# Halving the last chunk of each block's gather in two graph-attention layers of a three-layer GNN kernel

## The chip, the cores and the metric

One core of a Trainium2 chip runs the whole program. The metric is the device time of one execution in microseconds (us).

## What is computed

The input is a graph of 6250 nodes with 256 features and 100000 edges (`src`, `dst`, sorted by `dst`). There are three attention layers: two layers of a transformer-like GNN without edge types ("untyped", layers 0 and 1), and one with 64 edge types ("typed", layer 2).

```
h = x @ w_in + b_in
for l in range(2):                                  # the untyped layers
    xn = layernorm(h)
    q, k, v = xn @ wq[l] + bq[l], ...               # 8 heads of 32
    scores = einsum('ehd,ehd->eh', q[dst], k[src]) * scale       # an edge list with self loops
    attn = softmax over the edges with the same dst
    agg = segment_sum(attn * v[src], dst)
    h = h + agg @ wo[l] + bo[l]
    h = h + gelu(layernorm(h) @ w1[l] + b1[l]) @ w2[l] + b2[l]
```

The typed layer adds a row per edge type to k[src], has 4 heads, no feed-forward part, and ends with a layer normalisation.

## The kernel before

The nodes are sorted by their number of incoming edges and cut into 49 blocks of 128, one node for each partition. A block needs as many **slots** as its fullest node has edges. Four slots are a **chunk** (CH = 4), six chunks at most are a **round** (CPS = 6); a block has one round, but for two blocks that have two. A chunk is always whole: with 17 edges on its fullest node a block gathers 20 slots.

GpSimd (POOL in the profile) gathers: `gather_round` issues one indirect DMA for each slot, which brings for each of 128 nodes the row of one neighbour from `kv_dram`, 256 words of K and 256 of V, 256 KB in all, into the tile `kv` (L1255). `kv` holds two rounds. A chunk's gather waits for `used` (TensorE has summed this chunk two rounds ago) and for `taken` (VectorE has seen this chunk of the round before land). GpSimd also fetches the block's own rows (`gather_nodes`, L1235) and scatters the finished K and V rows of block b - 5 into the next layer's table (`scatter`, L1219), ahead of block b's gathers; the scatter waits for `recq`, ScalarE's last copy into `rec_out` (L1747).

VectorE (DVE) then goes over the block three times. `scores`: for each chunk `landed(c)` waits for its DMAs and counts up `taken`; `products(c)` multiplies K by the query in place (L1319); `head_sums(c-1)` adds up the heads of the chunk before (L1324). `maxima` (L1374 to L1379) subtracts the maxima for ScalarE's exponential. Then come the residual and the statistics of blocks b - 1 and b - 2 (`second`, L1492 in layer 0, L1494 in layer 1, waits for the feed-forward sum `f2`), and `weigh` multiplies V by the weights in place, chunk by chunk (L1424).

TensorE (PE) adds V's slots up in PSUM: `sums` has a loop over the chunks, four matmuls with the identity in each (L1870; the profile has two rows for each matmul, and two weight loads on PEld), and L1873 closes the sum. In the next iteration follow the feed-forward matmuls of block b - 2 (`feed_forward`, L1945, 32 rows; `feed_out`, L1958), the projections, and again `sums`. ScalarE (ACT) takes the sums (L1638), does the eight gelus (`hidden`, L1710), the exponential, and the copies into the record (`record`, L1745 to L1747).

The engines run one iteration for each block, in program order, and meet at semaphores; no planner sorts anything. How many rounds and chunks a block has comes from a small table that the first part of the kernel works out on the chip, `block_table`, two words a block; every engine reads a word of its copy `block_row` at the start of an iteration (L397).

Of the kernel before, what the change touches and what calls it, by code (L numbers as in the profile page):

```python
# [29 lines left out]
KMAX = NB + E // W  # L30
TYPES = 64
# [42 lines left out]
class Passed:  # L74
# [7 lines left out]
    def wait(self):  # L82
        self.eng.reg_add(self.count, self.count, self.by)
        self.eng.wait_ge(self.semaphore, self.eng.snap(self.count, min_val=1))
# [19 lines left out]
def build(nc, x, src, dst, edge_type_64, w, out):  # L104

    with ExitStack() as ctx:
# [17 lines left out]
        block_table = dram("block_table", [NB, 2], I32)  # L124
# [30 lines left out]
        block_row = sb("block_row", [1, NB * 2], I32)  # L155
# [7 lines left out]
        w_qkv = [sb(f"w_qkv{l}", [P, KD, 3 * D]) for l in range(3)]  # L163
# [29 lines left out]
        prod = sb("prod", [P, D])  # L193
        acc = sb("acc", [P, D])
# [76 lines left out]
        bt_out = carve(2, I32)  # L271
# [93 lines left out]
        ]  # L365
        later_loads = [
# [12 lines left out]
        for c, k in enumerate("kvq"):  # L379
            later_loads.append((w_qkv[2][:, :, c * D:(c + 1) * D], of_rows(w[f"L1_gnn_W{k}"])))  # L380
        later_loads.append((w_o[2][:], of_rows(w["L1_gnn_Wo"])))


        class Blocks:
# [9 lines left out]
            def next(self, b):  # L394

                sl = slice(2 * b, 2 * b + 1) if isinstance(b, int) else bass.ds(2 * b, 1)
                both = self.eng.value_load(block_row[0:1, sl], min_val=1, max_val=KMAX * PACKED + CPS)  # L397
# [10 lines left out]
        class Later:  # L408
# [7 lines left out]
            def next(self, b):  # L416
                at = 2 * b + 1
                sl = slice(at, at + 1) if isinstance(b, int) else bass.ds(at, 1)
                earlier = self.eng.value_load(block_row[0:1, sl], min_val=0, max_val=KMAX - NB)
# [80 lines left out]
        with nc.Block() as block:  # L500
# [151 lines left out]
            def _(dve):  # L652
# [124 lines left out]
                def block_sizes():  # L777
# [12 lines left out]
                    ceil_div(b0[:, 3:4], b0[:, 2:3], CPS)  # L790

                    step(nc.vector.tensor_scalar(b0[:, 4:5], b0[:, 3:4], -1.0, -float(CPS), ALU.add, ALU.mult))
                    step(nc.vector.tensor_tensor(b0[:, 4:5], b0[:, 4:5], b0[:, 2:3], ALU.add))
                    step(nc.vector.tensor_scalar(b0[:, 5:6], b0[:, 3:4], -1.0, float(PACKED), ALU.add, ALU.mult))
                    nc.vector.tensor_tensor(bt_out[0:NB, 0:1], b0[:, 4:5], b0[:, 5:6], ALU.add)
# [283 lines left out]
        for l in range(3):  # L1079
# [46 lines left out]
            with nc.Block() as block:  # L1126
                @block.sync
                def _(sp):
                    if not typed:
                        sp.dma_start(w_1, of_rows(w["L0_gnn_w1"][l])).then_inc(s["wload"], 16)  # L1130
                        sp.dma_start(w_2, of_rows(w["L0_gnn_w2"][l])).then_inc(s["wload"], 16)
                    looked_up, scored = Passed(sp, s["to_exp"]), Passed(sp, s["scaled"])
# [76 lines left out]
                def _(pool):  # L1209
# [38 lines left out]
                    def gather_round(u, k, chunks_left):  # L1248
                        def gather(c):
# [4 lines left out]
                            for slot in range(c * CH, (c + 1) * CH):  # L1254
                                pool.indirect_dma_start(  # L1255
# [802 lines left out]
```

## Time and profile before

| | |
|---|---|
| median of three runs | 6420.99 us (6406.24 to 6423.1) |
| the profiled execution: its time | 6426.95 us |
| its span in the profile | 6424.9 us |
| gathers of neighbour rows (L1255) | 2616, 872 in each layer |
| busy: PE, DVE, POOL, ACT | 62%, 55%, 46%, 30% of the span |

The profiled execution's time is 2.0 us over its span and 6.0 us over the median of the runs. Times in rows are microseconds from the span's start, unless they are marked ns. "x26" is a number of instructions, "issue" is time in which the engine waited for nothing that the profile shows, and the name behind "<-" is what ended an idle stretch.

### The profile page before, as it was taken

How to read it: one execution, taken by the hardware profiler on the slowest of the kernel's cores; microseconds unless marked ns; L12 is line 12 of the kernel's file. 1: busy time of each engine (PE TensorE's matmuls, PEld its weight loads, DVE VectorE, ACT ScalarE, POOL GpSimd, SP SyncE). 2: the span in 40 equal slices, each digit the busy share in tenths (PEclk: the TensorE clock that was granted, in tenths of full speed). 3: DMA queues.
4: the chain of work that ended last, by engine and by line, in shares of the span. 5: the costliest groups of instructions: out<-in, count | busy, mean ns of one | idle time of the engine just before them, and what ended most of it. 6: DMA issues, size and time to landing. Idle time of an engine off the chain costs nothing. (4 is left out here: it accounts for less than half of the span.)

```text
span 6424.9 us, 95711 instructions
## 1 busy us (share of the span) xinstructions
PE 3987.0 (62%) x17667; PEld 2921.0 (45%) x17668; DVE 3509.8 (55%) x5215; ACT 1924.9 (30%) x4404; POOL 2952.8 (46%) x2969
## 2 busy tenths in 40 slices
PE   8555455665666666565466566666666456666665
PEld 6222344544454444444354454444445345545544
DVE  6431445655555444355465555444436567777775
ACT  3332232222222222332222222222234222333433
POOL 0230435545444444244554444444425466666664
PEclk9777677777777777777777777777787667777777
DMA  3333545555554444344555555444435456665553
GB/s 123 128 115 81 158 128 163 161 156 154 151 151 138 147 147 140 113 134 138 171 159 157 157 154 143 138 141 141 141 99 153 123 168 174 183 173 172 170 173 108
DMA packets 384172, 935.62 MB, mean 146 GB/s; under 512 B 143749, under 2 KB 156255, under 8 KB 384105
## 3 DMA queue, kind: packets, MB, share of 16 engines
q0 software_dynamic: 232080, 751.31, 40.9%
q1 hardware_dynamic: 151708, 182.79, 8.8%
q10 hardware_dynamic: 320, 0.84, 0.0%
q8 instruction: 18, 0.29, 0.0%
q14 instruction: 46, 0.38, 0.0%
HBM read 791.63 MB, written 143.30 MB: 146 GB/s over the span
## 5 line engine op out<-in xcount | busy, mean ns | idle before, releaser
L1255 POOL DMA_INDIRECT kv<-kv_dram,idx x2616 | 2600.3, 994 | 1397.4 <-issue 770.5
L1870 PE MATMUL ps_acc<-kv,ident 128*128 x5232 | 1288.1, 408 | 49.3 <-issue 39.1
L1870 PEld LDWEIGHTS ps_acc<-kv,ident 128*128 128x128 f32 x5232 | 1074.2, 207 | 259.3 <-issue 95.6
L1324 DVE TENSOR_REDUCE sc<-kv 128x32 f32 (+2 forms) x654 | 791.2, 1213 | 362.2 <-issue 347.0
L1945 PE MATMUL ps_big<-xnaT,w_ffn 128*128 128x128 f32 x3136 | 524.5, 301 | 620.1 <-issue 616.5
L1319 DVE TENSOR_TENSOR kv<-kv,ps_q 128x1024 f32 x654 | 785.6, 1214 | 201.4 <-issue 197.8
L1958 PE MATMUL ps_w<-w_ffn,shared 128*128 128x256 f32 x1568 | 557.2, 531 | 390.8 <-ACT shared L1710 339.9
L1424 DVE TENSOR_TENSOR kv<-kv,ps_q x654 | 753.8, 1215 | 45.7 <-issue 36.3
L1945 PEld LDWEIGHTS ps_big<-xnaT,w_ffn 128*128 128x128 f32 x3136 | 446.7, 209 | 662.9 <-issue 651.1
L1958 PEld LDWEIGHTS ps_w<-w_ffn,shared 128*128 128x128 f32 x1568 | 426.0, 279 | 543.0 <-ACT shared L1710 399.0
L1638 ACT COPY agg<-ps_acc 128x256 f32<-128x256 f32 x147 | 54.8, 373 | 1949.9 <-remote 1054.3
L1219 POOL DMA_INDIRECT kv_dram<-rec_out,scatter_to x98 | 100.4, 1025 | 829.9 <-issue 829.9
L1710 ACT ACTIVATE shared<-ps_big,b 128x128 f32<-128x128 f32 x784 | 214.1, 382 | 545.3 <-remote 523.4
L477 PE MATMUL ps_t<-ident,xna 128*128 128x128 f32 x392 | 98.0, 338 | 412.6 <-issue 236.1
L489 PE MATMUL ps_kv<-w_qkv,xnbT 128*128 128x512 f32 x588 | 334.8, 698 | 0.0
L1311 DVE TENSOR_TENSOR kv<-kv,w_ffn x218 | 265.7, 1219 | 44.9 <-issue 33.0
L1235 POOL DMA_INDIRECT rec_in<-in_x,node_at x49 | 50.0, 1020 | 475.1 <-issue 475.1
L1492 DVE TENSOR_TENSOR rec_out<-h,ps_w 128x256 f32 (+1 forms) x49 | 20.6, 421 | 450.4 <-PE ps_w L1958 403.1
L477 PEld LDWEIGHTS ps_t<-ident,xna 128*128 128x128 f32 x392 | 47.9, 160 | 472.9 <-issue 248.6
L1494 DVE TENSOR_TENSOR h<-h,ps_w 128x256 f32<-128x256 f32 x49 | 20.6, 421 | 435.9 <-PE ps_w L1958 407.3
L456 ACT ACT_TABLE_LOAD x96 | 123.2, 1283 | 372.5 <-DVE mv L1515 353.6
L477 PE MATMUL ps_t<-ident,agg 128*128 128x128 f32 x294 | 84.7, 356 | 224.9 <-issue 179.3
(235 smaller groups left out, 5183.3 us busy)
## 6 DMA issues: line engine op xcount, KB each, us to landing
rec_dram<-rec_out SPq DMA_DIRECT2D x98, 512.0 KB
rec_in<-rec_dram SPq DMA_DIRECT2D x98, 512.0 KB
kv<-kv_dram,idx POOLq DMA_INDIRECT x2616
rec_by_node<-rec_in SPq DMA_DIRECT2D x49, 512.0 KB
windows<-kv SPq DMA_DIRECT2D x49, 384.0 KB
kv_dram<-rec_in SPq DMA_DIRECT2D x49, 256.0 KB
rec_out<-in_x SPq DMA_DIRECT2D x48, 128.0 KB
w_ffn<-in_L_gnn_w SPq DMA_DIRECT2D x4, 1024.0 KB, 6.6
```

The lines of the kernel that those rows point to most:

```text
L456: nc.scalar.activation(sd[:], mv[:, :, 1], ACT.Sqrt, bias=eps_col[:]).then_inc(done, 1)
L477: mm = nc.tensor.transpose(to[:, c, :], of[:, c * P:(c + 1) * P], ident[:])
L489: mm = nc.tensor.matmul(to, ofT[:, c, :], wt[:, c, a:z], start=False, stop=(c == KD - 1))
L1255: pool.indirect_dma_start(kv[:, u * W + slot, :], None, kv_dram[l], bass.IndirectOffsetOnAxis(ap=idx[:, u, slot:slot + 1], axis=0)).then_i ...
L1311: nc.vector.tensor_tensor(at, at, rel_of(k, c).unsqueeze(2).broadcast_to([P, CH, H, DH]), ALU.add).then_inc(s["relk"], 1)
L1319: nc.vector.tensor_tensor(at, at, q, ALU.mult).then_inc(s["mul"], 1)
L1324: nc.vector.tensor_reduce(scw[:, slice(c * CH * H, (c + 1) * CH * H) if isinstance(c, int) else bass.ds(c * (CH * H), CH * H)].rearrange(" ...
L1424: nc.vector.tensor_tensor(at, at, wt.unsqueeze(3).broadcast_to([P, CH, H, DH]), ALU.mult).then_inc(s["weighted"], 1)
L1710: nc.scalar.activation(gT[:, f, :], ps_big[:, f // 4, (f % 4) * P:(f % 4 + 1) * P], ACT.Gelu, bias=b_1[:, l, f:f + 1]).then_inc(s["g"], 1)
L1870: mm = nc.tensor.matmul(ps_acc[:, 0:D], ident[:], at[:, :, slot, :].rearrange("p a d -> p (a d)"), start=False, stop=False, skip_group_che ...
L1945: mm = nc.tensor.matmul(to, w_1[:, c, f * P:(f + 1) * P], xnaT[:, c, :], start=(c == 0), stop=(c == KD - 1))
L1958: mm = nc.tensor.matmul(to, gT[:, f, :], w_2[:, f, :], start=False, stop=(f == KF - 1))
```

## The change

It concerns layers 0 and 1 alone.

- The block table has a third word: how many half chunks (two slots) the block's last round needs. Its value is worked out by seven more small VectorE instructions in the first part of the kernel.
- GpSimd gathers the chunks but the first of a block's last round in two parts: slots 0 and 1, then, under an `If`, slots 2 and 3. Only the block's very last chunk can lack its second half. The first chunk of a round is always whole.
- VectorE's `landed(c)` waits for 32 or 64, as many as the chunk has DMAs in flight, worked out by four more register operations. Products go to a tile of their own, `work`, with room for two chunks, and before `products(c)`, from c = 2 on, it waits for the `head_sums` that read the same half of `work`. All vector instructions stay four slots wide; what stands in slots that were not gathered gets a weight of zero.
- TensorE sums whole chunks in the loop, and the last chunk behind it: one matmul, then three more or one more under an `If`/`Else`.
- GpSimd, VectorE and TensorE each read the new word (`halves_of`) once in each block: TensorE between its last transposes and `sums`, VectorE between the start of the block and `scores`, GpSimd ahead of its gathers.
- To make room for `work` (8 KB a partition), layer 1's output weights for q, k and v, `w_qkv[2]`, share the tile of `w_qkv[0]`. They are loaded at the start of layer 0 (three transfers of 256 KB, behind the two of the feed-forward weights) and no longer in the first part.

```diff
-        w_qkv = [sb(f"w_qkv{l}", [P, KD, 3 * D]) for l in range(3)]
+        w_qkv = [sb(f"w_qkv{l}", [P, KD, 3 * D]) for l in range(2)]
+        w_qkv.append(w_qkv[0])
...
+        work = sb("work", [P, 2, CH * D])
...
+        def halves_of(eng, b):
+            return block_word(eng, b, 2, 1, 2 * CPS)
...
+                    if l == 0:
+                        for to, of in next_qkv:
+                            sp.dma_start(to, of).then_inc(s["wload"], 16)
...
-                            for slot in range(c * CH, (c + 1) * CH):
-                                pool.indirect_dma_start(
-                                    kv[:, u * W + slot, :], None, kv_dram[l],
-                                    bass.IndirectOffsetOnAxis(ap=idx[:, u, slot:slot + 1], axis=0)).then_inc(
-                                        kv_sem[c], 16)
+                            if c == 0 or typed:
+                                rows(c, range(c * CH, (c + 1) * CH))
+                                return
+                            rows(c, range(c * CH, c * CH + CH // 2))
+                            with pool.If(left > 2 * c + 1):
+                                rows(c, range(c * CH + CH // 2, (c + 1) * CH))
+                                pool.nop()
...
+                            dve.reg_alu(rows_due, halves, 2 * c, ALU.subtract)
+                            dve.reg_alu(rows_due, rows_due, 2, ALU.min)
+                            dve.reg_alu(rows_in, rows_due, 1, ALU.max)
+                            dve.reg_mul(landed_by, rows_in, LANDED // 2)
+                            landings[c].wait(landed_by)
                         dve.sem_inc(s["taken"], 1)
...
-                            nc.vector.tensor_tensor(at, at, q, ALU.mult).then_inc(s["mul"], 1)
+                            nc.vector.tensor_tensor(at if typed else worked(c), at, q, ALU.mult).then_inc(s["mul"], 1)
...
                             if c:
-                                landed(c)
+                                landed(c, halves)
+                            if c >= 2 and not typed:
+                                dve.wait_ge(s["score"], chunk0 + c - 1)
+                                settle(dve)
...
-                    def sums(k, chunk0, filled):
+                    def sums(k, chunk0, filled, halves=None):
...
+                            with pe.If(filled > 1):
+                                whole_chunks(filled - 1)
+                                pe.nop()
+                            pe.wait_ge(s["weighted"], chunk0 + filled)
+                            add(filled - 1, range(CH // 2 - 1))
+                            with pe.If(halves > filled * 2 - 1):
+                                add(filled - 1, range(CH // 2 - 1, CH)).then_inc(s["used"], 1)
+                                pe.nop()
+                            with pe.Else():
+                                add(filled - 1, range(CH // 2 - 1, CH // 2)).then_inc(s["used"], 1)
+                                pe.nop()
```

VectorE, in the loop over a layer's blocks, the fourth chunk of `scores`; "ISA" is a fused register operation, `l0_kv3` counts this chunk's DMAs, `mul` the products and `score` the head sums that are done. Before:

```order
L1348 COMPARE_AND_BRANCH
L83 ISA
L1319 ISA [waits l0_kv3]
L1319 TENSOR_TENSOR kv<-kv,ps_q 128x4x256
L1322 ISA
L1324 ISA [waits mul]
L1324 TENSOR_REDUCE sc<-kv 128x32
L1348 UNCONDITIONAL_BRANCH
```

And now:

```order
L1392 COMPARE_AND_BRANCH
L1329 ISA
L1376 ISA [waits l0_kv3]
L1361 ISA [waits score]
L1361 TENSOR_TENSOR work<-kv,ps_q 128x1024
L1364 REGISTER_ALU
L1366 TENSOR_REDUCE sc<-work 128x32 [waits mul]
L1392 UNCONDITIONAL_BRANCH
```

The product has a second wait ahead of it, for the head sums issued just before it, and one more row of registers.

TensorE, between the transposes that end an iteration and the first chunk of `sums`. Before:

```order
L477 MATMUL ps_t_w<-ident,xnb 128x128
L1863 ISA
L1864 MATMUL ps_acc<-acc_scaled,ident 128x256 [waits scaled]
L1866 UNCONDITIONAL_BRANCH
L1866 ISA
L1870 ISA [waits weighted]
```

And now:

```order
L486 MATMUL ps_t_w<-ident,xnb 128x128
L391 ISA
L391 TENSOR_LOAD block_row
L391 ISA x2
L1909 ISA
L1910 MATMUL ps_acc<-acc_scaled,ident 128x256 [waits scaled]
L1928 COMPARE_AND_BRANCH
L1921 UNCONDITIONAL_BRANCH
L1921 ISA
L1916 ISA [waits weighted]
```

The read of the table's word, with its register rows, stands between the last transpose and the sum's first matmul, and a branch behind it.

GpSimd, the second chunk of a round. Before:

```order
L1263 COMPARE_AND_BRANCH
L1250 REGISTER_ALU
L1255 DMA kv<-kv_dram,idx 128x512 [waits used,taken]
L1255 DMA kv<-kv_dram,idx 128x512 x3
L1263 UNCONDITIONAL_BRANCH
```

And now:

```order
L1288 COMPARE_AND_BRANCH
L1273 REGISTER_ALU
L1267 DMA kv<-kv_dram,idx 128x512 [waits used,taken]
L1267 DMA kv<-kv_dram,idx 128x512
L1281 COMPARE_AND_BRANCH
L1267 DMA kv<-kv_dram,idx 128x512 x2
L1281 UNCONDITIONAL_BRANCH
L1288 UNCONDITIONAL_BRANCH
```

A compare and a branch stand inside each chunk now.

## Rows read from the trace of the kernel before

**Rows 1.** The page's part 1: busy us, share of the span, instructions.

```profile
PE 3987.0 (62%) x17667; PEld 2921.0 (45%) x17668; DVE 3509.8 (55%) x5215; ACT 1924.9 (30%) x4404; POOL 2952.8 (46%) x2969
```

**Rows 2.** Windows, one per part: stretch, length, busy per engine, PEclk, DMA share, GB/s.

```profile
0.00:645.00 645.00, 414.25 (x1735) 236.74 (x1736) 266.20 (x662) 208.02 (x541) 102.28 (x108) 0.79 0.36 112
645.00:2704.00 2059.00, 1283.23 (x5327) 950.61 (x5327) 1036.83 (x1511) 562.03 (x1283) 929.06 (x973) 0.77 0.50 146
2704.00:4785.00 2081.00, 1277.59 (x5327) 949.03 (x5327) 1053.75 (x1560) 572.21 (x1328) 924.12 (x967) 0.77 0.49 144
4785.00:6424.90 1639.90, 1011.90 (x5278) 784.59 (x5278) 1152.98 (x1482) 582.61 (x1252) 997.30 (x921) 0.73 0.55 160
```

**Rows 3.** The page's part 5: group, count, busy us, mean ns, idle before, releaser.

```profile
L1255 POOL DMA_INDIRECT kv<-kv_dram,idx x2616 | 2600.3, 994 | 1397.4 <-issue 770.5
L1870 PE MATMUL ps_acc<-kv,ident 128*128 x5232 | 1288.1, 408 | 49.3 <-issue 39.1
L1492 DVE TENSOR_TENSOR rec_out<-h,ps_w 128x256 f32 (+1 forms) x49 | 20.6, 421 | 450.4 <-PE ps_w L1958 403.1
L1494 DVE TENSOR_TENSOR h<-h,ps_w 128x256 f32<-128x256 f32 x49 | 20.6, 421 | 435.9 <-PE ps_w L1958 407.3
```

**Rows 4.** Timeline of POOL, one iteration of layer 1: start, us, idle before.

```profile
4386.75 1.03 POOL L1219 DMA_INDIRECT kv_dram<-rec_out,scatter_to  x1 [4.96 <-issue]
4388.18 0.96 POOL L1255 DMA_INDIRECT kv<-kv_dram,idx  x1 [0.41 <-issue]
4389.45 0.95 POOL L1255 DMA_INDIRECT kv<-kv_dram,idx  x1 [0.30 <-issue]
...
4406.97 0.94 POOL L1255 DMA_INDIRECT kv<-kv_dram,idx  x1 [0.30 <-issue]
...
4427.80 1.03 POOL L1219 DMA_INDIRECT kv_dram<-rec_out,scatter_to  x1 [5.13 <-issue]
```

**Rows 5.** Timeline of PE in the same iteration, around the gathers' end.

```profile
4391.77 3.15 PE L1945 MATMUL ps_big<-xnaT,w_ffn 128*128 128x128 f32 x26
...
4398.96 0.37 PE L1945 MATMUL ps_big<-xnaT,w_ffn 128*128 128x128 f32 x1 [1.74 <-issue]
...
4404.64 0.37 PE L477 MATMUL ps_t<-ident,agg 128*128 128x128 f32 x1 [2.46 <-issue]
```

**Rows 6.** Timeline of all engines in the same iteration, from the slow stretch on.

```profile
4401.11 1.22 DVE L1324 TENSOR_REDUCE sc<-kv  x1 [4.40 <-issue]
...
4411.22 2.17 ACT L1710 ACTIVATE shared<-ps_big,b 128x128 f32<-128x128 f32 x8 [7.39 <-remote]
...
4411.64 6.76 PE L1958 MATMUL ps_w<-w_ffn,shared 128*128 128x256 f32 x16 [1.73 <-ACT shared L1710]
...
4418.44 0.42 DVE L1494 TENSOR_TENSOR h<-h,ps_w 128x256 f32<-128x256 f32 x1 [7.81 <-PE ps_w L1958]
...
4425.63 7.14 PE L1870 MATMUL ps_acc<-kv,ident 128*128 x32
```

**Rows 7.** Windows of single iterations (one L1439 to the next), columns as in rows 2.

```profile
2893.00:2927.20 34.20, 21.02 (x99) 15.71 (x98) 16.36 (x27) 11.57 (x27) 13.60 (x15) 0.80 0.46 135
4306.00:4347.00 41.00, 25.08 (x107) 18.34 (x106) 19.70 (x31) 11.58 (x27) 17.15 (x18) 0.79 0.46 139
2121.30:2156.70 35.40, 25.09 (x106) 18.26 (x105) 19.54 (x29) 11.32 (x26) 17.06 (x19) 0.81 0.52 155
3890.90:3932.80 41.90, 27.69 (x114) 20.60 (x113) 23.45 (x33) 11.57 (x27) 20.89 (x22) 0.80 0.56 160
3844.10:3890.90 46.80, 28.57 (x115) 21.10 (x115) 23.46 (x34) 11.57 (x27) 21.33 (x23) 0.74 0.52 145
```

**Rows 8.** Timeline of POOL in the 35.40 us iteration of rows 7.

```profile
2139.09 0.95 POOL L1255 DMA_INDIRECT kv<-kv_dram,idx  x1 [3.41 <-ACTq L1632]
```

**Rows 9.** Rows of two lines on the queues: count, then ns min/median/max.

```profile
L397 PEldq TENSOR_LOAD <-block_row x147: 298/304/487, 645.7 to 6377.6; - x147
L1348 DVEq COMPARE_BRANCH  x1206: 1/47/1398, 667.2 to 6384.1; - x173
```

**Rows 10.** The page's part 6: transfers, KB each, median us from issue to landing.

```profile
w_ffn<-in_L_gnn_w SPq DMA_DIRECT2D x4, 1024.0 KB, 6.6
```

More of the change, by code:

```diff
@@ L30 @@
 KMAX = NB + E // W
+WORDS = 3
 TYPES = 64
@@ L80, in __init__, with wait @@
         eng.reg_mov(self.count, 0)
-    def wait(self):
-        self.eng.reg_add(self.count, self.count, self.by)
+    def wait(self, by=None):
+        self.eng.reg_add(self.count, self.count, self.by if by is None else by)
         self.eng.wait_ge(self.semaphore, self.eng.snap(self.count, min_val=1))
@@ L365, in build @@
         ]
+        next_qkv = []
         later_loads = [
@@ L1246, in gather_nodes, with gather_round, rows @@
                         pick(pool, b % RING, do, range(RING))
-                    def gather_round(u, k, chunks_left):
+                    def gather_round(u, k, left):
+                        def rows(c, slots):
+                            for slot in slots:
+                                pool.indirect_dma_start(
+                                    kv[:, u * W + slot, :], None, kv_dram[l],
+                                    bass.IndirectOffsetOnAxis(ap=idx[:, u, slot:slot + 1], axis=0)).then_inc(
+                                        kv_sem[c], 16)
                         def gather(c):
@@ L1262, in gather_round @@
                                 continue
-                            with pool.If(chunks_left > c):
+                            with pool.If(left > (c if typed else 2 * c)):
                                 gather(c)
+                                pool.nop()
                             pool.nop()
@@ L1604, in iteration @@
                             weigh(k, chunk0, filled)
+                    rows_due, rows_in, landed_by = (dve.alloc_register(f"l{l}_{r}") for r in (
+                        "rows_due", "rows_in", "landed_by"))
                     extras = dve.alloc_register(f"l{l}_extras")
@@ L1865, in sums, with add, whole_chunks @@
                                          skip_group_check=True)
-                        with pe.Fori(0, filled) as c:
-                            pe.wait_ge(s["weighted"], chunk0 + c + 1)
+                        def add(c, slots):
                             at = chunks[:, one((k % 2) * CPS + c), :, D:2 * D]
-                            for slot in range(CH):
+                            for slot in slots:
                                 mm = nc.tensor.matmul(ps_acc[:, 0:D], ident[:], at[:, :, slot, :].rearrange(
                                     "p a d -> p (a d)"), start=False, stop=False, skip_group_check=True)
-                            mm.then_inc(s["used"], 1)
+                            return mm
+                        def whole_chunks(n):
+                            with pe.Fori(0, n) as c:
+                                pe.wait_ge(s["weighted"], chunk0 + c + 1)
+                                add(c, range(CH)).then_inc(s["used"], 1)
+                        if halves is None:
+                            whole_chunks(filled)
+                        else:
+                            with pe.If(filled > 1):
[9 more added lines that the diff above has]
+                                pe.nop()
                         nc.tensor.matmul(ps_acc[:, 0:32], ident_b[:], zeros_b[:, 0:32], start=False, stop=True,
@@ L2011, in iteration @@
                         if exists(b):
-                            sums(k, chunk0, filled)
+                            sums(k, chunk0, filled, None if typed else halves_of(pe, b))
                     pe.sem_inc(s["used"], 2 * CPS)
```

50 lines of the change are left out of this document (31 added, 19 removed).

## The prediction

> **What bounds the kernel now.** I read the page's engine totals first [rows 1]: no engine is busy for more than 62% of the span, so a loop of waits sets the time, not an engine. The windows by part [rows 2] give layers 0 and 1, which alone change in their loops, 2059 and 2081 us; the first part (645 us) and layer 2 (1640 us) keep nearly all their work. The groups [rows 3] then show that VectorE sat 403 + 407 us in front of the feed-forward sum (L1492, L1494), some 8 us a block. VectorE has slack there; the chain through TensorE and ScalarE has not.
>
> One iteration of layer 1 on GpSimd [rows 4] shows the loop. From one scatter (4386.75) to the next (4427.80) it takes 41.05 us. First come 16 gathers without a break, one each 1.25 us, until 4407.91, 21.2 us after the scatter. The last 19.9 us hold no gather of a neighbour: the scatter waits for ScalarE's record. What ScalarE and TensorE do meanwhile explains why this is serial. TensorE runs 26 of the 32 feed-forward rows in 3.15 us, and then, still under the gathers, single matmuls up to 2.5 us apart that wait for nothing the profile shows [rows 5]. VectorE has the same gaps (4.40 us ahead of a reduction) [rows 6]. A branch on VectorE's queue takes 47 ns in the median and up to 1398 [rows 9]. I call this the slow stretch: some 6 us after a run of gathers begins, the sequencers crawl until 3 to 4 us behind the last gather. ScalarE's gelus start at 4411.22, 3.3 us after the last gather ended, and TensorE's L1958 at 4411.64 [rows 6]; from the gelus to the next scatter it is 16.6 us. So the loop is: gathers, 3.3 us of draining, 16.6 us of chain that can't begin before.
>
> The windows of single iterations [rows 7] show the price of gathers: 34.20 us with 12, 41.00 with 16, 46.80 with 20. But 35.40 us also occurs with 16, and 41.90 with 20. In the 35.40 us iteration GpSimd paused for 3.41 us after 12 gathers [rows 8]; the slow stretch lifted in the pause, and the chain ran beside the last four gathers.
>
> **The change, part by part.** How often is a half chunk saved? Not the trace but the inputs tell. From the degrees of the drawn graph, sorted as the kernel does, the blocks need 218 chunks (872 slots, a third of the trace's 2616 gathers [rows 3]), and 23 of 49 blocks of a layer end in a chunk of which two slots suffice: 2 blocks of three chunks, 8 of four, 9 of five, 4 of six. Two layers: 46 half chunks, 92 gathers fewer. At 1.25 us each this is 115 us of GpSimd's time, the most the gathers can give straight.
>
> *Gathers.* Where the chain starts behind the last gather, two fewer are worth 2.5 us in full. All 16 four-chunk blocks are of this kind (40.0 us), and the 4 three-chunk ones (10.0 us). Of the 18 five-chunk blocks I count 6 or 7 with the long period: 6.5 x 2.5 = 16 us; in the other 11.5 an early pause has already let the chain start, and I take 0.7 us each, 8 us. For the 8 six-chunk blocks I take 2 us each, 16 us. Sum: 90 us off. Bounds: 45 (only half of it reaches the chain) and 115.
>
> *TensorE.* Four matmul rows fewer on a half chunk: 32 rows take 7.14 us [rows 6], so 0.9 us off. But reading the table's word stands ahead of every block's sum: 0.30 us for the load [rows 9] and its register rows, which no row of rows 1 to 10 prices alone; I take 0.7 us together with the branch behind it, bounds 0.3 and 1.2. On the 46 blocks the two cancel. On the other 52 the feed-forward rows start 0.7 us later. That matters because TensorE runs them in 3.15 us just before the slow stretch, and each row that falls into it crawls, and what is left at its end stands ahead of the chain. Between 0 (all done by then anyway, as with three chunks) and 2 us a block I take 0.7: 36 us on, bounds 0 and 100.
>
> *VectorE.* The same word's load, and a wait for the head sums just issued, which lets the product start some 0.3 us later from the third chunk on: 1 to 2 us a block, 100 to 200 us in all, behind 8 us of slack a block [rows 3]. If the slack were gone they would cost that. I take 5 us, for the six-chunk blocks. The tensor instructions themselves are as wide as before (1.22 us [rows 6]) and cost nothing new; that the output is another tile I price at zero.
>
> *GpSimd.* A compare and a branch more in each chunk, 0.05 us each while all is well [rows 9] and hidden under a gather. In the slow stretch an instruction costs up to 0.7 us and more, so GpSimd falls behind its own gathers and pauses sooner. A pause of 3.4 us shortened an iteration by 5.6 us (35.40 against 41.00) [rows 7, 8]; shorter ones bring nothing that I can see. That may hit some of layer 0's 17 iterations of four chunks: I take a third of them by 4.4 us, 25 us off; bounds 0 and 150 (all 34 of both layers).
>
> *Layer start and first part.* Three 256 KB transfers stand ahead of layer 0's first slot table; a pair of 1024 KB ones lands 6.6 us after issue in the median [rows 10], so 768 KB more and their issues cost 3 to 4 us once. Seven tiny VectorE instructions: 1 us. Together 5 us on.
>
> The branches draw on a rule as well. The Trainium skill, "Runtime: NRT & Kernel Launch", section "Instruction fetch mechanics", says that a taken branch whose target is outside the two pages held forces a fetch, and stalls. By that rule this change, with longer loop bodies and more branches on three engines, would lose time everywhere, and the sum below would turn positive. The trace does not agree outside the slow stretch: VectorE's branches have a median of 47 ns [rows 9]. Inside it, it can't be told from the traffic.
>
> **Sum.** -90 + 36 + 5 - 25 + 5 = -69 us. Against the profiled execution's own 6427 us that is 6358, against the median of the runs, 6421, it is 6352. I predict 6350.
>
> **The rivals.**
> 1. *The pause becomes the rule.* GpSimd's added rows make it pause after the third chunk in most blocks, and the chain then runs under the last gathers. 34 iterations by 4.4 us is 150 us, with half of the gathers' 90 still to be had: 6421 - 150 - 45 = 6226, some 6230. For it: both lengths stand side by side in layer 0 [rows 7]. Against: 41.00 us without a pause is what layer 1 repeats.
> 2. *The sequencers eat it (slower).* Place: the start of the slow stretch. TensorE's word load pushes the feed-forward rows into it in all 98 blocks, and VectorE's added waits reach the chain in the long blocks. 98 x 1.5 us is 147, less 90: 6480. It decides as soon as the added start delay costs more than 0.9 us a block over all 98 (90 / 98). For it: 26 rows ran in 3.15 us and the six behind them took some 7 [rows 5]. Against: in the row iteration TensorE had finished these rows 9 us before the slow stretch ended.
> 3. *Nothing to be seen.* The burst is hidden by pauses in five- and six-chunk blocks, and the 50 us that the three- and four-chunk blocks give are paid back by the delays: 6421 within 19 us.
>
> **How the numbers follow.** This kernel can be told from no change at about 0.3%, 19 us. My forecast, gathers less some delay, 20 to 130 us faster: 0.58. Rival 1: 0.16. Rival 3: 0.12. Rival 2: 0.14. So faster 0.74, within 0.3% 0.12, slower 0.14. The range reaches from 6250 (the pause in part of the blocks) to 6430: it leaves out the far half of rival 1 and most of rival 2, about 2 in 10.
>
> **What would show it.** The profile after should have 2524 gathers and 92 x 2 rows fewer of the identity matmul. A four-chunk iteration of layer 1 whose gathers are 14 should take 38.5 us in place of 41.00, one with 16 about 41 to 42. The gelus should start 3.3 us behind the last gather in both. Wrong would be the forecast if full four-chunk blocks are longer by over 2 us (TensorE late), if VectorE no longer waits at `second` (its slack gone), or if iterations of 16 gathers fall to 35 us (rival 1). Layer 2 should keep its 1640 us within 5; if it doesn't, something outside my account moved.

## The result and the profile after

The changed kernel takes 6475.6 us in the median of 20 runs (6453.9 to 6497.9), the kernel before 6456.9 us in 20 runs beside it (6405.1 to 6487.6). The ratio on record is 1.0045, with a 95% interval from 1.0026 to 1.0064: 0.45% slower, some 29 us (the two medians alone are 19 us apart, a ratio of 1.0029). The forecast was 6350, faster. The first three runs of before had a median of 6421; its own runs spread over some 80 us, so only ratios against runs of before beside them are compared below. In microseconds I give them on 6421: 0.1% is 6.4 us. One run of an experiment below (pe_dve_early) took 8419 us, in the slow state, and is left out of its ratio.

The page of the changed kernel, part 1, answers to [rows 1]:

```profile
PE 3931.1 (61%) x17475; PEld 2860.2 (44%) x17476; DVE 3526.8 (54%) x5222; ACT 1923.6 (30%) x4404; POOL 2861.3 (44%) x2877
```

GpSimd's busy time falls by 91.5 us, TensorE's by 56, VectorE's rises by 17. Less work, more time: the loop of waits has grown. The windows by part, as in [rows 2]:

```profile
0.00:645.00 645.00, 410.21 (x1735) 235.77 (x1736) 267.32 (x669) 207.71 (x541) 102.27 (x108) 0.80 0.35 112
645.00:2732.00 2087.00, 1249.25 (x5231) 916.72 (x5231) 1044.69 (x1511) 562.26 (x1283) 884.27 (x927) 0.77 0.46 138
2732.00:4826.00 2094.00, 1271.35 (x5231) 930.15 (x5231) 1060.86 (x1560) 572.88 (x1328) 879.66 (x922) 0.78 0.46 138
4826.00:6484.30 1658.30, 1000.25 (x5278) 777.51 (x5278) 1153.94 (x1482) 580.73 (x1252) 995.09 (x921) 0.74 0.55 158
```

Layer 0 is 28 us longer, layer 1 13 us, layer 2 18 us. Layer 2 does the same work as before. From its first block to its last I read 1567.5 us before and 1586.5 after, and in the first four experiments below 1559.4 to 1575.1: that part scatters by itself, and this profile drew the long end. The two profiled executions are 60 us apart, twice what the ratio gives.

Part 5 of the page, against [rows 3]:

```profile
L1267 POOL DMA_INDIRECT kv<-kv_dram,idx x2524 | 2508.2, 994 | 1406.0 <-issue 750.5
L1916 PE MATMUL ps_acc<-kv,ident 128*128 x5040 | 1287.9, 419 | 64.5 <-issue 51.6
L2024 PE MATMUL ps_w<-w_ffn,shared 128*128 128x256 f32 x1568 | 572.3, 541 | 703.7 <-ACT shared L1756 552.8
L2011 PE MATMUL ps_big<-xnaT,w_ffn 128*128 128x128 f32 x3136 | 439.7, 286 | 330.9 <-issue 327.1
L1756 ACT ACTIVATE shared<-ps_big,b 128x128 f32<-128x128 f32 x784 | 215.0, 379 | 950.5 <-remote 900.2
```

and two groups of the same part for the kernel before:

```profile
L1945 PE MATMUL ps_big<-xnaT,w_ffn 128*128 128x128 f32 x3136 | 524.5, 301 | 620.1 <-issue 616.5
L1710 ACT ACTIVATE shared<-ps_big,b 128x128 f32<-128x128 f32 x784 | 214.1, 382 | 545.3 <-remote 523.4
```

The 92 gathers are gone. The first feed-forward rows crawl less: 331 us idle ahead of L2011, where L1945 had 620. The gelus wait more, 950 us against 545. And VectorE still waits at `second` (the feed-forward sum), in the groups of its lines:

```profile
L1536 DVE TENSOR_TENSOR rec_out<-h,ps_w 128x256 f32 (+1 forms) x49 | 20.6, 421 | 301.3 <-PE ps_w L2024 298.0 <-issue 3.3
L1538 DVE TENSOR_TENSOR h<-h,ps_w 128x256 f32<-128x256 f32 x49 | 20.6, 421 | 301.4 <-PE ps_w L2024 299.7 <-issue 1.7
```

That is 6 us a block, where [rows 3] had 8.

The windows of single iterations of layer 1, GpSimd alone, show where it was won and lost: a four-chunk block beside 14 gathers, one beside 16, a five-chunk block beside 18, one beside 20.

```profile
4556.90:4594.70 37.80, 13.26 (x14) 0.80 0.46 136
4198.50:4239.50 41.00, 15.14 (x16) 0.79 0.46 139
3855.60:3899.90 44.30, 17.01 (x18) 0.77 0.47 139
3446.00:3493.60 47.60, 18.93 (x20) 0.75 0.48 141
```

Two gathers fewer shorten a four-chunk iteration by 3.2 us. But a five-chunk iteration with 18 gathers takes 44.3 us, more than the 41.90 that one with 20 took before [rows 7]. Before, GpSimd stood still for 2 to 4 us in mid-burst, mostly after gather 12 or 16, in 33 of the 74 iterations of blocks 11 to 47 (I count two gathers that start over 3.2 us apart, 1.25 being the rule). In the changed kernel it does so in 10. The short iterations were the ones with such a pause.

What a pause waits for can be read too. Here is one of before, from the timeline of POOL in a five-chunk block of layer 1, and from the timeline of PE the sum beside it, which frees the slots of this burst:

```profile
3931.93 0.97 POOL L1255 DMA_INDIRECT kv<-kv_dram,idx  x1 [0.31 <-issue]
...
3950.73 0.96 POOL L1255 DMA_INDIRECT kv<-kv_dram,idx  x1 [0.30 <-issue]
3955.69 0.94 POOL L1255 DMA_INDIRECT kv<-kv_dram,idx  x1 [4.01 <-ACTq L1632]
```

```profile
3928.43 8.87 PE L1870 MATMUL ps_acc<-kv,ident 128*128 x40
```

The fifth chunk's gathers wait for `used`. By its matmul records TensorE is through with all five chunks at 3937.30. But the trace's semaphore events, which these views don't print, have `used` rise only at 3941.39 for the fourth chunk and at 3954.82 for the fifth, and GpSimd's wait for it ends at 3954.84. (L1632, which the row names, is where ScalarE counts up the same semaphore, for chunks that a block lacks.) All 33 pauses of before end like this: the gather starts 0.9 us behind a wait for `used` that ended within 0.05 us of a rise of it. In the changed kernel 5 of the 10 do. So GpSimd does not stop by itself: a signal of TensorE's reaches it late.

The timeline of POOL in one iteration of layer 1, against [rows 4]:

```profile
4399.85 1.03 POOL L1235 DMA_INDIRECT kv_dram<-rec_out,scatter_to  x1 [5.36 <-issue]
4402.97 0.96 POOL L1267 DMA_INDIRECT kv<-kv_dram,idx  x1 [2.09 <-PE ps_acc L1916]
...
4421.74 0.95 POOL L1267 DMA_INDIRECT kv<-kv_dram,idx  x1 [0.30 <-issue]
...
4436.26 1.02 POOL L1251 DMA_INDIRECT rec_in<-in_x,node_at  x1 [13.57 <-issue]
```

The first gather comes 3.12 us behind the scatter; it was 1.43 us. It waited for TensorE's sum, which frees the first chunk's slots, behind GpSimd's own load of the word. In the median over the layers' iterations the distance rose from 1.34 to 2.54 us. What TensorE and ScalarE did there, from the timelines of both:

```profile
4396.38 0.44 PE L486 MATMUL ps_t<-ident,xna 128*128 128x128 f32 x2 [1.26 <-ACT xna L1761]
4396.87 0.44 PE L486 MATMUL ps_t_w<-ident,xnb 128*128 128x128 f32 x2
4397.74 0.69 PE L1910 MATMUL ps_acc<-acc_scaled,ident 128*128 128x256 f32 x2 [0.44 <-issue]
4398.49 8.75 PE L1916 MATMUL ps_acc<-kv,ident 128*128 x32
...
4407.11 3.82 PE L2011 MATMUL ps_big<-xnaT,w_ffn 128*128 128x128 f32 x32
...
4425.85 2.17 ACT L1756 ACTIVATE shared<-ps_big,b 128x128 f32<-128x128 f32 x8 [15.80 <-remote]
```

The word's load opens a gap of 0.44 us ahead of the sum. The 32 sum rows take 8.75 us; they took 7.14 [rows 6]. All 32 feed-forward rows then run in one piece and by their records, whose ends are modelled, are done at 4410.93. Yet the gelus start at 4425.85, 3.16 us behind the last gather's end (4421.74 + 0.95). They are not slow to start: by the semaphore events `f1`, which TensorE raises for them behind each half of its rows, rose at 4425.83 and 4425.99. In 36 of the 38 iterations of layer 1 from block 11 on, the first gelu starts within 0.1 us of such a rise. It is again TensorE's signal that comes late, as with `used`. The windows around the sum tell why the sum is longer (PEclk is the third number from the end):

```profile
4396.00:4398.00 2.00, 1.13 (x5) 0.67 (x6) 2.00 (x2) 1.87 (x6) 0.00 (x0) 1.00 0.10 27
4398.00:4402.00 4.00, 3.94 (x11) 2.89 (x11) 3.24 (x5) 1.42 (x5) 1.03 (x1) 0.57 0.47 192
4402.00:4411.00 9.00, 9.00 (x60) 8.19 (x58) 7.84 (x7) 1.66 (x2) 6.20 (x7) 1.00 0.53 147
```

TensorE's granted clock was 0.57 for the sum's first rows, close to the lower of its two levels (1.2 of 2.4 GHz), after two idle gaps of 1.26 and 0.44 us.

### The profile page after: what moved, and what is told of

The parts are those of the page before. It is cut to its first block and busy times, and to the rows that moved or that the text cites. A ratio compares the mean times of both kernels' runs of the same rounds, so it can differ in the third digit from the quotient of the medians.

```text
span 6484.3 us, 96926 instructions
## 1 busy us (share of the span) xinstructions
PE 3931.1 (61%) x17475; PEld 2860.2 (44%) x17476; DVE 3526.8 (54%) x5222; ACT 1923.6 (30%) x4404; POOL 2861.3 (44%) x2877
## 5 line engine op out<-in xcount | busy, mean ns | idle before, releaser
L1267 POOL DMA_INDIRECT kv<-kv_dram,idx x2524 | 2508.2, 994 | 1406.0 <-issue 750.5
L2024 PE MATMUL ps_w<-w_ffn,shared 128*128 128x256 f32 x1568 | 572.3, 541 | 703.7 <-ACT shared L1756 552.8
L1366 DVE TENSOR_REDUCE sc<-work 128x32 f32<-128x1024 f32 (+1 forms) x436 | 528.2, 1215 | 473.8 <-issue 472.2
L1361 DVE TENSOR_TENSOR work<-kv,ps_q 128x1024 f32<-128x1024 f32 x436 | 523.7, 1220 | 407.5 <-issue 378.5
L2011 PE MATMUL ps_big<-xnaT,w_ffn 128*128 128x128 f32 x3136 | 439.7, 286 | 330.9 <-issue 327.1
L2011 PEld LDWEIGHTS ps_big<-xnaT,w_ffn 128*128 128x128 f32 x3136 | 393.7, 198 | 345.6 <-issue 333.8
L1353 DVE TENSOR_TENSOR kv<-kv,w_ffn x218 | 266.0, 1220 | 43.9 <-issue 38.5
L1366 DVE TENSOR_REDUCE sc<-kv 128x16 f32 (+1 forms) x218 | 264.5, 1213 | 12.3 <-DVE kv L1361 11.0
L1361 DVE TENSOR_TENSOR kv<-kv,ps_q 128x1024 f32 x218 | 264.3, 1212 | 1.9 <-DVE kv L1353 0.2
L486 PEld LDWEIGHTS ps_t<-ident,xna 128*128 128x128 f32 x392 | 46.9, 157 | 432.8 <-ACT xna L1761 189.7
L1910 PE MATMUL ps_acc<-acc_scaled,ident 128*128 128x256 f32 x306 | 126.0, 500 | 169.8 <-DVE acc_scaled L1432 124.1
L491 PE MATMUL ps_w<-bias_parts,ones_rows 3*128 3x256 bf16 x245 | 73.4, 300 | 236.1 <-ACT xnaT L960 115.6
```

Of the source, the lines that this page charges most:

```text
L486: mm = nc.tensor.transpose(to[:, c, :], of[:, c * P:(c + 1) * P], ident[:])
L1267: pool.indirect_dma_start(kv[:, u * W + slot, :], None, kv_dram[l], bass.IndirectOffsetOnAxis(ap=idx[:, u, slot:slot + 1], axis=0)).then_i ...
L1353: nc.vector.tensor_tensor(at, at, rel_of(k, c).unsqueeze(2).broadcast_to([P, CH, H, DH]), ALU.add).then_inc(s["relk"], 1)
L1361: nc.vector.tensor_tensor(at if typed else worked(c), at, q, ALU.mult).then_inc(s["mul"], 1)
L1366: nc.vector.tensor_reduce(scw[:, slice(c * CH * H, (c + 1) * CH * H) if isinstance(c, int) else bass.ds(c * (CH * H), CH * H)].rearrange(" ...
L1910: nc.tensor.matmul(ps_acc[:, 0:D], ident[:], acc_scaled[:], start=True, stop=False, skip_group_check=True)
```

## The experiments

Three theories of the loss. **Late words**: TensorE's and GpSimd's table words are loaded on the path and make the burst begin later. **Work tile**: VectorE's separate tile, with its wait, costs. **Burst shape**: the shorter bursts alone lose the pauses. Later a fourth, **pause**: what counts is whether GpSimd stops in mid-burst. Edits are shown shortened.

Each ratio is to runs of before in the same session. In the session of the first four, before had a median of 6421; in the three sessions of the others it had 6326 to 6334.

**words_only**: two unused word loads added to the kernel before.

```
+ GpSimd, between scatter and first gather: spare = value_load(block_row[2 * b + 1])
+ TensorE, directly ahead of sums(...):     spare = value_load(block_row[2 * b + 1])
```

> The kernel before, with one more table word loaded and not used by GpSimd between scatter and first gather, and by TensorE ahead of each block's sum. No halving, no work tile. Theory 'late words' (the two loads stand on the path: GpSimd's first gather comes 0.9 us later behind the scatter, and TensorE's gap ahead of the sum lowers its granted clock there): 60 to 100 us slower than before, ratio 1.009 to 1.016, and in layer 1 many iterations with sum rows over 600 ns. Theory 'work tile' (VectorE's separate tile and its added wait cost it): ratio 0.998 to 1.002. Theory 'burst shape' (only the shorter burst takes away the pause behind gather 16): ratio 0.998 to 1.002 too.

Measured: 1.0211 (1.0163 to 1.026), some 135 us. Scatter to first gather 2.34 us in the median, 7 pauses. That is more than late words asked for; neither of the others can explain any of it.

**work_only**: the tile, its wait and the later weights, added to the kernel before.

```
- tensor_tensor(at, at, q, ALU.mult)
+ tensor_tensor(work[:, c % 2], at, q, ALU.mult)     # and head_sums reads it
+ if c >= 2: wait_ge(s["score"], chunk0 + c - 1)
```

> The kernel before, with the products in a tile of their own, the wait for the head sums two chunks back, and the third layer's weights loaded later into the first's tile. No halving, no added word. 'Late words': ratio 0.997 to 1.003, pauses of 3.7 us behind gather 16 stay in layer 1's five-chunk blocks (period 42 to 43 us). 'Work tile': 60 to 100 us slower, ratio 1.009 to 1.016. 'Burst shape': ratio 0.997 to 1.003.

Measured: 1.0001 (0.9972 to 1.0029), 35 pauses. The tile and its wait cost nothing that shows.

**pe_word_early**: in the changed kernel TensorE's word stands beside the block's others.

```
  counts = blocks.next(b)
+ halves = halves_of(pe, b)
  ...
- sums(k, chunk0, filled, halves_of(pe, b))
+ sums(k, chunk0, filled, halves)
```

> The changed kernel, with TensorE's word loaded beside the block's other words, ahead of the hidden state's turning, and no longer directly ahead of the sum. 'Late words': sum rows over 600 ns in layer 1 fall from 196 to under 60, the five-chunk halved blocks from 44.3 us to about 42.5, total 30 to 60 us less than the changed kernel: ratio 0.995 to 1.000 to before. 'Work tile' and 'burst shape': ratio stays at 1.003 to 1.006.

Measured: 0.9973 (0.9943 to 1.0004). That is 0.7% less than the changed kernel. Sum rows over 600 ns in layer 1 fell from 196 to 33 (before: some 30), as expected. The five-chunk halved blocks of layer 1 stayed at some 44 us, which was not: the first gather was still 2.32 us behind the scatter, and there were 6 pauses.

**pool_word_early**: the same with GpSimd's word alone, moved ahead of the node gather.

> The changed kernel, with GpSimd's word loaded ahead of the node gather, no longer between scatter and first gather. 'Late words': scatter to first gather falls from 3.1 us in the median to 2.2 or less, total 30 to 80 us less than the changed kernel: ratio 0.992 to 0.999. If the start of the burst is set by TensorE's sum alone, ratio stays at 1.003 to 1.006 and the distance at about 3 us. 'Work tile': ratio 1.003 to 1.006.

Measured: 1.0037 (1.0005 to 1.0069), first gather at 2.22 us, 14 pauses. The distance fell as late words had it, the time did not: with TensorE's word still late the move gains nothing that can be told. Either lateness is enough.

**pe_word_only**: TensorE's unused word alone, on the kernel before.

> The kernel before, with one more table word loaded and not used by TensorE alone, directly ahead of each block's sum. With both engines' words it was 1.021. If TensorE's word makes that loss (late sum, lower granted clock at its head, later release of the first chunk to GpSimd): ratio 1.012 to 1.021, and the pauses over 2 us in GpSimd's bursts of blocks 11 to 47 fall from 33 to under 12. If GpSimd's word made it: ratio 0.998 to 1.005 and the pauses stay.

Measured: 1.022 (1.0185 to 1.0256), 141 us, 8 pauses, first gather at 2.23 us. Layer 0 had only some 60 sum rows over 600 ns (before: some 40) and is 75 us longer than in the profile of before, layer 1 had 213 and is 38 us longer. So the lowered clock is not what makes the loss.

**late_word**: GpSimd's unused word alone, on the kernel before.

> The kernel before, with one more table word loaded and not used by GpSimd alone, between scatter and first gather. If the later start of the burst is what takes the pauses away, whoever causes it: scatter to first gather 2.0 us or more, pauses of blocks 11 to 47 from 33 to under 12, ratio 1.010 to 1.022. If only TensorE's later sum does: the pauses stay, ratio 0.998 to 1.005.

Measured: 1.0188 (1.0164 to 1.0211), 121 us, with TensorE's sum as early as before (0.11 us behind the start of the last turning row, as there) and only 26 and 38 sum rows over 600 ns in layers 0 and 1. Two pauses are left. The timeline of POOL in a five-chunk block of layer 1, and below it that iteration's window:

```profile
3516.54 1.03 POOL L1219 DMA_INDIRECT kv_dram<-rec_out,scatter_to  x1 [5.19 <-issue]
3518.86 0.96 POOL L1255 DMA_INDIRECT kv<-kv_dram,idx  x1 [1.30 <-PE ps_acc L1875]
...
3542.65 0.94 POOL L1255 DMA_INDIRECT kv<-kv_dram,idx  x1 [0.30 <-issue]
```

```profile
3518.70:3566.00 47.30, 19.22 (x21) 0.75 0.48 143
```

The gathers run 2.32 us behind the scatter and then 20 in a row without a stop (the window's 21st is the first of the next burst), and the iteration takes 47.3 us instead of 41.90 [rows 7]. The later start of the burst by 1 us is enough, whoever causes it. (The profile names TensorE as releaser here; the load on GpSimd's own queue is what was added.)

The semaphore events show why the pauses go. Take the 15 five-chunk blocks of layer 1, and the time from the first gather to the end of GpSimd's wait for the fifth chunk's `used`, in the median. It is 22.9 us in before (14 of the 15 bursts pause), 20.5 in words_early (6 pause), 15.6 in pe_word_only (2), 14.2 in pe_delay_only (none) and 7.9 here (none). The 16 gathers ahead of that chunk last 20 us, 16 by 1.25: a signal that is there by then causes no pause.

**pe_delay_only**: the kernel before, eight waits that are already met ahead of the sum, no load.

```
+ for _ in range(8):
+     pe.wait_ge(s["query"], 1); settle(pe)
```

> The kernel before, with eight waits that are already met, and no load, on TensorE's queue ahead of each block's sum: some 0.8 us of its sequencer's time. If any delay of the sum by 0.8 us is what costs: ratio 1.014 to 1.024, like TensorE's late word (1.022), scatter to first gather over 2 us in the median, and pauses nearly gone. If it is the load as such: ratio 0.998 to 1.005.

Measured: 1.0337 (1.0313 to 1.0361), 216 us, above the expected range; first gather at 2.67 us, 6 pauses. The timeline of PE ahead of a sum:

```profile
4369.69 0.44 PE L477 MATMUL ps_t_w<-ident,xnb 128*128 128x128 f32 x2
4370.99 0.69 PE L1864 MATMUL ps_acc<-acc_scaled,ident 128*128 128x256 f32 x2 [0.86 <-issue]
```

From the start of the last turning row to the sum I read 1.14 us in the median, against 0.11 before and 0.70 with the word: a delay of 1.0 us, not of the 0.8 that I had meant. So the load as such is not needed: a delay of 0.6 us costs 2.2%, one of 1.0 us 3.4%.

**words_early**: the changed kernel with all three words early.

> The changed kernel, with the third word loaded on all three engines (TensorE, GpSimd, VectorE) beside the block's first two. If only TensorE's place counts: the same as with TensorE's alone moved, ratio 0.994 to 1.000. If VectorE's load ahead of its first product and GpSimd's behind the scatter cost 1 us a block each as well: ratio 0.985 to 0.993, with the pauses behind gather 16 back in the five-chunk blocks.

Measured: 0.9899 (0.9868 to 0.993), first gather at 1.38 us. That is 1.5% or 94 us less than the changed kernel, and inside the second of the two expected ranges, but without the pauses that I expected with it: 12, not 30. The shorter bursts lose some of them by themselves.

**pe_dve_early**: TensorE's and VectorE's words early, GpSimd's late.

> The changed kernel with TensorE's and VectorE's words loaded early and GpSimd's still behind the scatter. TensorE's alone gave 0.9973, all three 0.9899. If the rest is GpSimd's 0.9 us ahead of the first gather: ratio 0.996 to 0.998 and scatter to first gather 2.2 to 2.3 us. If it is VectorE's load ahead of its first product: 0.989 to 0.992. If both share: 0.993 to 0.995.

Measured: 0.9942 (0.9927 to 0.9958). It lies between TensorE's move alone (0.9973) and all three (0.9899): both others seem to have a share, 20 and 28 us by the ratios, though neighbouring intervals overlap a little.

**paced3**: as words_early, and GpSimd waits ahead of a block's fourth chunk for the first gelu.

```
+ if c == 3 and not typed:
+     with pool.If(b >= DEPTH + 1):
+         pool.wait_ge(s["g"], pace)      # pace grows by KF gelus a block
```

> As words_early, and GpSimd waits ahead of a block's fourth chunk until ScalarE has made the first gelu of the block three back. If the missing pause is what costs (theory 'pause'): iterations of four chunks fall to 35 to 36 us, of five to 39 to 40, in both layers; total 6150 to 6250, ratio 0.955 to 0.975. If the pauses seen were only a sign of something else that was early: the forced wait costs 2 to 4 us a block, ratio 1.00 to 1.03.

Measured: 0.9336 (0.9297 to 0.9374), beyond what was expected. Iterations with 14 or 16 gathers take 34 us, with 18 or 20 some 36 to 38.

**before_paced3**: the same wait in the kernel before.

> The kernel before, with the same wait ahead of a block's fourth chunk. Theory 'pause': four chunks 35 to 36 us, five 39 to 40 us, total 6180 to 6260, ratio 0.962 to 0.978; beside the halved kernel with the same wait it says what the halves are worth once the chain no longer waits behind them: 46 halves by at most 2.5 us, and less than 40 us if they are hidden. If the pause is only a sign: ratio 1.00 to 1.03.

Measured: 0.9396 (0.9363 to 0.9429), beyond what was expected here too. One added wait makes the kernel before 6% faster. The halves are then worth 0.6%, some 39 us of the 115 that they could be, and not clear of noise: the two intervals overlap.

**after_paced3**: the wait in the changed kernel, its words late.

> The changed kernel with its words late, and GpSimd's wait ahead of the fourth chunk until the first gelu. If the late words cost what they cost by taking away the pauses (theory 'pause'), the forced pause gives nearly all back: ratio 0.934 to 0.940, within 0.6% of the kernel with early words and the same wait (0.9336). If they cost because the sum itself is later on the chain (theory 'later sum'): the 1.5% between late and early words stays, ratio 0.946 to 0.952.

Measured: 0.9409 (0.9385 to 0.9432), 0.73% over paced3, between the two ranges and nearer to the first: with the pause forced, about half of the 1.5% between late and early words goes, the other half stays as plain lateness.

**paced3_g8**: paced3, waiting for the eighth gelu.

> Early words, the wait ahead of the fourth chunk lasts until the eighth gelu in place of the first, some 1.8 us longer. If the gathers behind the pause disturb the chain, the longer pause keeps the gelus and part of the second feed-forward rows clear: same or up to 1% less than 0.9336. If GpSimd's burst is again the bound: blocks of five and six chunks 1.8 us longer, ratio 0.937 to 0.943.

Measured: 0.9179 (0.9161 to 0.9196). The pauses are 5.4 us long instead of 3.6, and it is 1.6% better, more than expected: gathers that start again right behind the first gelu do slow the chain.

**paced2**: the wait ahead of the third chunk.

> Early words, GpSimd's wait ahead of the third chunk in place of the fourth. Theory 'pause' with a slow stretch that begins some 6 us into a run of gathers: the chain starts 5 us earlier, blocks of three chunks fall from 36 to about 33 us, but 8 to 16 gathers behind the pause slow the chain in blocks of four to six: those 1 to 3 us longer than with the wait ahead of the fourth; ratio 0.925 to 0.955. If the length of what follows a pause does not matter: 0.91 to 0.925.

Measured: 0.8904 (0.8885 to 0.8923). Both expected ranges were a miss: iterations with 18 or 20 gathers fell too, to 32.9 and 36.4 us, though 10 or 12 gathers follow the pause.

**paced2_g8**: the wait ahead of the third chunk, until the eighth gelu; the fastest of all.

> Early words, GpSimd's wait ahead of the third chunk until the eighth gelu (paced2: the first gelu, 0.8904). If gathers right behind a short pause slow the chain that starts in it: 0.875 to 0.889. If the burst of blocks of five and six chunks is the bound with a pause so early: 0.892 to 0.905.

Measured: 5574.1 us beside 6333.6, ratio 0.8821 (0.8794 to 0.8848), inside the first range. The page's part 1, and the timelines of POOL and ACT in a four-chunk block of layer 1:

```profile
PE 3830.3 (69%) x17475; PEld 2806.5 (50%) x17476; DVE 3532.4 (64%) x5222; ACT 1936.9 (35%) x4404; POOL 2872.6 (52%) x2877
```

```profile
3487.23 1.03 POOL L1235 DMA_INDIRECT kv_dram<-rec_out,scatter_to  x1 [0.71 <-issue]
3488.84 0.96 POOL L1267 DMA_INDIRECT kv<-kv_dram,idx  x1 [0.59 <-issue]
...
3497.61 0.95 POOL L1267 DMA_INDIRECT kv<-kv_dram,idx  x1 [0.30 <-issue]
3503.45 0.94 POOL L1267 DMA_INDIRECT kv<-kv_dram,idx  x1 [4.90 <-issue]
...
3518.35 1.03 POOL L1235 DMA_INDIRECT kv_dram<-rec_out,scatter_to  x1 [1.58 <-issue]
```

```profile
3500.24 2.17 ACT L1768 ACTIVATE shared<-ps_big,b 128x128 f32<-128x128 f32 x8 [5.73 <-remote]
```

Eight gathers, 4.90 us without one, eight more beside the chain. The gelus start 1.68 us behind the eighth gather's end (3498.56), 11.4 us after the first gather began; in the changed kernel it was 22.9 us. The windows of single iterations, a four-chunk block with 16 and one with 14 gathers, and a three-chunk block:

```profile
3489.10:3518.95 29.85, 15.06 (x16) 0.94 0.61 187
3757.30:3786.00 28.70, 13.24 (x14) 0.88 0.61 187
2433.20:2461.40 28.20, 11.57 (x12) 0.88 0.55 164
```

The mean period of an iteration by the gathers beside it, blocks 11 to 47 of both layers, in us (the columns from words_early on, and late_word, are from sessions in which before took some 1.5% less):

| gathers | before | late_word | words_only | after | words_early | paced3 | paced2_g8 |
|---|---|---|---|---|---|---|---|
| 14 (after halving; 16 without), x16 | 39.7 | 40.1 | 40.7 | 37.8 | 36.8 | 34.5 | 28.7 |
| 16, x20 | 40.2 | 39.8 | 40.8 | 41.0 | 39.9 | 34.1 | 30.2 |
| 18 (20 without), x18 | 43.2 | 46.6 | 46.3 | 43.7 | 41.9 | 36.2 | 33.3 |
| 20, x12 | 42.8 | 46.4 | 46.9 | 46.0 | 44.3 | 38.1 | 36.3 |
| 22 (24 without), x8 | 48.1 | 50.5 | 49.7 | 50.5 | 46.9 | 42.4 | 40.7 |

Late words cost the iterations that had 20 gathers before 3 to 4 us; they are the ones that had pauses behind gather 16. Halving alone (words_only to after) gives 2.9 us where 14 run and 2.6 where 18 do, the 2.5 of two gathers.

## Why the prediction was wrong

**The sum.** I had gathers -90, TensorE +36, VectorE +5, GpSimd -25, first part +5. The sum comes to -69, the ratio to +29. It failed at one step above all: the pauses. It had the gathers begin when they did and pause more often; the change made them begin later and pause less. The runs give, in the same order of cause:

- *Gathers.* From words_only to the changed kernel, with the words late in both, the time falls by 1.66%: 106 us, net of VectorE's late word. With the words early (work_only to words_early) it is 1.0%, 65 us; with a forced pause, 39 us. Each of the three is good to some 30 us. My 90 lies among them, and the mechanism was right: an iteration of layer 1 with 14 gathers took 37.1 to 39.7 us, 38.1 in the mean (38.5 forecast), one with 16 took 41.1 in the mean (41 to 42 forecast), the gelus start 3.2 us behind the last gather (3.3 forecast). What was wrong is the line on five-chunk blocks: "an early pause has already let the chain start, and I take 0.7 us each". It took the pause as given, and the change removed it.
- *TensorE.* The delay itself was sized well: 0.6 us (0.7 taken). Its consequence was not. I let it push feed-forward rows into the slow stretch; they left it instead (idle ahead of them 620 to 331 us): the rows moved back by some 0.6 us, the burst by 1.2 in the median. The sum's first chunk also frees the slots of the first gather, which I named nowhere: I asked what stands behind the load on TensorE, and not who waits for what the sum frees. Alone it costs 141 us, outside the bounds 0 and 100.
- *GpSimd.* This is the step that failed worst. I priced "a compare and a branch more in each chunk", and left out that GpSimd too loads the third word, in the one place where nothing hides it, between scatter and first gather. Alone: +121 us. And the sign of the pauses was wrong: -25 for more pauses, with bounds 0 and -150; they fell from 33 to 10. The mechanism was too: I had GpSimd fall behind its own gathers over the added rows. In the traces the pause is the wait for `used`, and [rows 8] already named a line that raises this semaphore, ACTq L1632.
- *VectorE.* 1 to 2 us a block behind 8 us of slack: the slack fell by 2 us a block and stayed at 6. The tile and its wait are free (1.0001), as priced. Its late word may cost some 20 us (0.9973 to 0.9942, intervals overlapping), against 5.
- *First part.* The first block of layer 0 starts at 665.8 us, before at 666.4: nothing, for 5.

The two words' lateness does not add up: 141 and 121 alone, 135 together. Once the pauses are gone they can't be lost again. (135 less 106 is the 29 by construction, as 106 was taken from the same two ratios; it is no check.)

None of the three signs by which I said the forecast would be wrong showed: full four-chunk blocks are 0.8 us longer, `second` still waits, 16 gathers did not fall to 35 us. They all looked at four-chunk blocks or at slack, and the loss is in blocks of five and six: full five-chunk ones went from 42.8 to 46.0 us.

**The rivals.** Rival 2 gave 6480 and 1.5 us a block; measured are 6475.6, and 135 / 98 = 1.4 us a block from the two words. That 6480 comes so near is luck: it was 59 us over 6421, and measured are 29 over the runs beside it, which stood 36 us higher. The price a block was right and "the sequencers eat it" was not: neither feed-forward rows nor VectorE's waits are where it goes. Rival 1, the pause as the rule, did not come about by itself, and had its worth too small: forced, it gives not the 3% of that rival but 6% to 12%. I named the lever and took it for something that the change might pull by chance.

**The page's rule.** The Trainium skill, "Runtime: NRT & Kernel Launch", section "Instruction fetch mechanics", has taken branches outside the held pages stall, and by it, as I read it in the prediction, longer bodies cost time everywhere. Here eight met waits without a branch cost 3.4%, and work_only, with rows added on VectorE, nothing. Where the added rows stand decided, not how many there are. A fetch stall was not separated from the traffic in any run.

**What stays open.** What holds TensorE's signals back while gathers run, and why the fifth chunk's comes earlier when the burst begins 1 us later, is not shown. As the ends of matmuls are modelled, it is not shown either whether the rows were done and the signal hung, or the rows themselves were late. Half of the changed kernel's ten pauses are not accounted for; many rows of its queue inside the slow stretch are missing from the trace. That the pause is what shortens the iteration is shown by forcing it.

## What to carry to other kernels

A register load costs little where its engine's queue is ahead of the work, and far more where the engine is what a loop waits for: load a block's words together, early, and ask of each added row not only what its engine does next but who waits for what it frees. Where a burst of transfers holds up everything else, count the pauses in it before and after, and try a wait that puts one where the chain needs it: here a single line in the kernel before was worth 6%, over ten times what the change moved. An averaged slack says nothing about a good coincidence that the change may end; where two lengths stand side by side for the same work, find what makes the short one before pricing anything else. And where an engine seems to stop for nothing, look up when the semaphore that its queue waits for rose, and not only when the work behind it ended.

## What the runs showed of the hardware

- While gathers run without a pause, TensorE's semaphores rise long after its matmul records end: `used` at 3954.82 for rows recorded up to 3937.30 (before), `f1` at 4425.83 and 4425.99 for rows recorded up to 4410.93 (after). What waits for them starts at once: the gelus at 4425.85. With 4.90 us between two gathers (paced2_g8) the gelus began 1.68 us behind the eighth.
- Eight waits that were already met put TensorE's sum off by 1.03 us together (1.14 against 0.11), 0.13 us each.
- A gap of 0.44 us ahead of the sum went with a granted clock of 0.57 over the next 4 us in this iteration; sum rows over 600 ns in layer 1 were some 30 before, 196 in the changed kernel, 33 with the word early.
- The kernel before took 6457 us in the median beside the changed kernel, 6421 in the first session of experiments and 6326 to 6334 in three others. The record gives the session of 6421 and that of 6326 the same chip number, so it doesn't show that this goes by the chip. In the profiles of kernels with the same code there, layer 2 took some 50 us less in the later sessions and the first part some 25.
